# Hybrid transformer block on one core: a logarithm folded into the row of maxima, and a new order in the first unit

## What is computed

```python
x = x + attn_a(layernorm(x))   # 16 heads of width 64, full softmax, own residual and layer norm
x = x + ffn(layernorm(x))      # 128 -> 512 -> relu -> 128
x = x + attn_b(layernorm(x))   # 8 heads of width 128, rope, causal softmax
x = x + ffn(layernorm(x))
# attn_a: softmax over keys of (Q K^T) * 64**-0.5 * adaptive_scale[head], times V, times Wo
# attn_b: softmax over keys of (rope(Q) rope(K)^T) / 128, masked, times V, times Wo
```

## Time and profile before

| | |
|---|---|
| median of 3 runs | 1948.1 us (1947.27 to 1948.55) |
| profiled execution, its own time | 1947.32 us |
| its span | 1945.5 us |
| lead of phase A | up to 53.77 us, the first scores |
| phase A's steps | 53.77 to 1217.57 us, the end of the last exponential |
| dense layer and lead of phase B | to 1292.1 us |
| phase B's steps and the end | 1292.1 to 1945.5 us |
| busy, whole span | PE 96%, ACT 86%, POOL 83%, DVE 73% |
| mean granted clock of TensorE | 0.986 of full speed |

### The profile page before, as it was taken

How to read it: one execution, slowest core, us unless ns; L and a number is a source line. 1 busy time by engine, 2 the same in 40 slices (tenths; PEclk the granted TensorE clock), 3 DMA queues, 4 the chain that set the end, 5 groups by cost and what they waited for, 6 DMA issues and landing times.

```text
span 1945.5 us, 55434 instructions
## 1 busy us (share of the span) xinstructions
PE 1873.1 (96%) x23343; PEld 1268.5 (65%) x23343; DVE 1414.1 (73%) x2613; ACT 1674.5 (86%) x1919; POOL 1612.9 (83%) x1025
## 2 busy tenths in 40 slices
PE   4899999999999999999999999779999999999998
PEld 2566666666666666666666666547776777767766
DVE  7787778778777877877877864566767767667642
ACT  4799999999999999999999999747777777777774
POOL 3799999999999999999999999358787787886752
PEclk8899999999999999999999999889999999999999
DMA  6101101100100100100100100100000000000000
GB/s 145 35 11 26 34 14 23 35 15 21 35 18 18 34 19 18 35 18 18 35 18 18 34 2 2 55 1 2 2 1 2 2 2 1 2 1 2 2 2 23
DMA packets 45032, 37.94 MB, mean 19 GB/s; under 512 B 8304, under 2 KB 44144, under 8 KB 44528
## 3 DMA queue, kind: packets, MB, share of 16 engines
q1 hardware_dynamic: 44304, 34.00, 7.4%
q10 hardware_dynamic: 480, 0.39, 0.1%
HBM read 8.15 MB, written 1.05 MB: 5 GB/s over the span
## 4 chain that ended last, share of the span: by engine, by line
PE 84%; ACT 6%; DVE 4%; issue 3%; POOL 2%; ACTq 0%; POOLq 0%; DVEq 0%
PE ST L1612 10%; PE ST L1613 10%; PE RING L1473 6%; PE OO L1554 6%; PE OO L1556 6%; PE OO L1553 6%; PE OO L1473 4%; PE ST L1773 3%; PE ST L1778 3%; PE ST L1779 3%; PE ST L1780 3%; ACT PR L783 3%; PE OO L1800 2%; PE OO L1802 2%; PE OO L1804 2%
## 5 line engine op out<-in xcount | busy, mean ns | idle before, releaser
L609 POOL TENSOR_TENSOR PAB<-PR,PAB 128x1024 f16<-128x1024 f32 x342 | 728.8, 2131 | 51.4 <-ACT PAB L785 33.7
L785 ACT ACTIVATE PAB<-ST,lift_cols,exp_scale 128x1024 f16<-128x1024 f32 x512 | 654.5, 1278 | 0.0
L1081 DVE TENSOR_REDUCE maxes<-RING 128x1 f32<-128x512 f32 x661 | 439.8, 684 | 141.3 <-PE RING L1473 140.7
L783 ACT ACTIVATE PR<-ST,lift_cols,exp_scale 128x1024 f32<-128x1024 f32 x342 | 435.9, 1275 | 36.4 <-PE ST L1613 35.7
L1553 PE MATMUL OO<-VP,PAB 128*128 128x66 f16 x4096 | 447.2, 192 | 2.2 <-POOL PAB L609 2.2
L1554 PE MATMUL OO<-VP,PAB 128*128 128x64 f16 x4096 | 447.7, 194 | 0.0
L1556 PE MATMUL OO<-VP,PAB 128*128 128x66 f16 x4096 | 445.7, 192 | 0.0
L1553 PEld LDWEIGHTS OO<-VP,PAB 128*128 128x128 f16 x4096 | 380.7, 96 | 76.7 <-issue 14.7
L1554 PEld LDWEIGHTS OO<-VP,PAB 128*128 128x128 f16 x4096 | 377.5, 97 | 61.6
L1612 PE MATMUL ST<-QL,KH 128*128 128x512 f16 x1024 | 389.2, 380 | 4.1 <-ACT PAB L785 2.4
L1613 PE MATMUL ST<-QH,KL 128*128 128x512 f16 x1024 | 388.8, 380 | 0.0
(11 more groups left out here) (305 smaller groups left out, 4006.7 us busy)
## 6 DMA issues: line engine op xcount, KB each, us to landing
KH<-HS SPq DMA_DIRECT2D x124, 64.0 KB, 2.0
QL<-HS SPq DMA_DIRECT2D x64, 64.0 KB, 2.0
QL<-LS SPq DMA_DIRECT2D x64, 64.0 KB, 2.1
QH<-HS SPq DMA_DIRECT2D x64, 64.0 KB, 2.0
KL<-LS SPq DMA_DIRECT2D x62, 64.0 KB, 2.1
X<-in_L_attn_a_x SPq DMA_DIRECT2D x4, 256.0 KB, 3.9
SHARED<-in_rope_cos SPq DMA_DIRECT2D x1, 1024.0 KB, 5.0
SHARED<-in_rope_sin SPq DMA_DIRECT2D x1, 1024.0 KB, 7.1
```

Source lines behind the costliest of these rows:

```text
L609: pool.tensor_tensor(PB[:, s, :], PRA[g % PR_SLOTS], PA[:, s, :], ALU.subtract).then_inc(p_low_ready, 1)
L783: act.activation(PRA[g % PR_SLOTS], ST[step % 2][:, :], ACT.Exp, bias=lift_cols[:, 0:1], scale=scale)
L785: act.activation(PA[:, step % SLOTS_A, :], ST[step % 2][:, :], ACT.Exp, bias=lift_cols[:, 0:1], scale=scale).then_inc(sa.exps, 1)
L1081: dve.reduce_max(maxes[:, i // BLOCKS, i % BLOCKS:i % BLOCKS + 1], bank[:, :], X_AXIS).then_inc(sa.ring_taken, 1)
```

## The change

1. **No bias in the exponentials.** The column `lift_cols` is gone, and all 1024 exponentials of phase A and 640 of phase B are issued without a bias operand; the scale column stays.
2. **The logarithm goes into the row.** `take_rows` no longer computes `row * rowmask` but `(row + lift) * rowmask`, with `lift` a column of one value per head, `lifts` or `lifts_b` (one small DVE instruction each, computed once). It is a scalar_tensor_tensor in place of a tensor_tensor, 64 times in phase A and 32 times in phase B.
3. **`mask_operands` moves** from just ahead of `low_block` to just ahead of `bound_heads`, early in DVE's stream.
4. **First unit.** PE computes the scores of step 1 right after those of step 0. Values and maxima alternate: first half of the values, two maxima, second half, two maxima (item numbers 21, 22, 23, 24, 25, 26).

The diff, without the part that only moves the scores into a function of their own, `scores_a`:

```diff
-VALUES_LEAD = ROWS_LEAD + 1
+VALUES_LEAD = (ROWS_LEAD + 1, ROWS_LEAD + 4)
+MAX_LEAD = (ROWS_LEAD + 2, ROWS_LEAD + 3, ROWS_LEAD + 5, ROWS_LEAD + 6)
...
-                act.activation(PRA[g % PR_SLOTS], ST[step % 2][:, :], ACT.Exp, bias=lift_cols[:, 0:1], scale=scale)
+                act.activation(PRA[g % PR_SLOTS], ST[step % 2][:, :], ACT.Exp, scale=scale)
                 wait(act, sa.pv, g - SLOTS_A + 1)
-                act.activation(PA[:, step % SLOTS_A, :], ST[step % 2][:, :], ACT.Exp, bias=lift_cols[:, 0:1],
-                               scale=scale).then_inc(sa.exps, 1)
+                act.activation(PA[:, step % SLOTS_A, :], ST[step % 2][:, :], ACT.Exp, scale=scale
+                               ).then_inc(sa.exps, 1)
...
-            dve.memset(lift_cols[:, 0:1], LIFT)
-            dve.memset(lift_cols[:, 1:2], LIFT_B)
...
+                dve.scalar_tensor_tensor(lifts[:, :], qk_up[:, 0, :], LIFT, qk_up[:, 1, :], ALU.mult, ALU.mult)
...
+            mask_operands()
             bound_heads()
...
-            def take_rows(s, bank, item, dst):
+            def take_rows(s, bank, item, dst, lift):
 
                 dve.wait_ge(s.ring_put, item + 1)
                 rows = bank[0:BT, 0:P].unsqueeze(1).broadcast_to((BT, BT, P))
-                dve.tensor_tensor(dst.rearrange("p (a c) -> p a c", c=P), rows, rowmask[:, :, :],
-                                  ALU.mult).then_inc(s.ring_taken, 1)
+                dve.scalar_tensor_tensor(dst.rearrange("p (a c) -> p a c", c=P), rows, lift, rowmask[:, :, :],
+                                         ALU.add, ALU.mult).then_inc(s.ring_taken, 1)
...
-            mask_operands()
             low_block(1, 0, O[0])
...
             for half in range(2):
-                n = VALUES_LEAD + half
+                n = VALUES_LEAD[half]
                 take_values_a(0, half, RING3[n % 3], n)
-            for i in range(4):
-                n = VALUES_LEAD + 2 + i
-                take_max_a(RING3[n % 3], n, i, 1)
+                for i in (2 * half, 2 * half + 1):
+                    n = MAX_LEAD[i]
+                    take_max_a(RING3[n % 3], n, i, 1)
...
+                if g != 1:
+                    scores_a(g)
                 if g == 0:
+                    scores_a(1)
                     for half in range(2):
-                        values_a(half, VALUES_LEAD + half, 0)
-                    for i in range(4):
-                        max_a(1, i, VALUES_LEAD + 2 + i)
+                        values_a(half, VALUES_LEAD[half], 0)
+                        for i in (2 * half, 2 * half + 1):
+                            max_a(1, i, MAX_LEAD[i])
```

More of the change, by code:

```diff
@@ L299, in build @@
         exp_scale_b = sb("exp_scale_b", [P, HB])
-        lift_cols = sb("lift_cols", [P, 2])
+        lifts_b = sb("lifts_b", [P, HB])
         RAW = sb("RAW", [P, 4 * HA * DA])
@@ L317, in build @@
         exp_scale = sb("exp_scale", [P, HA])
+        lifts = sb("lifts", [P, HA])
         AT = sb("AT", [P, BLK])
@@ L893, in _ @@
                 act.wait_ge(sbb.scores, g + 1)
-                act.activation(PRB[g % PR_SLOTS_B][:, c0:BLK], SB[g % 2][:, c0:BLK], ACT.Exp,
-                               bias=lift_cols[:, 1:2], scale=scale)
+                act.activation(PRB[g % PR_SLOTS_B][:, c0:BLK], SB[g % 2][:, c0:BLK], ACT.Exp, scale=scale)
                 wait(act, sbb.pv, g - SLOTS_B + 1)
-                act.activation(PAH[:, g % SLOTS_B, c0:BLK], SB[g % 2][:, c0:BLK], ACT.Exp,
-                               bias=lift_cols[:, 1:2], scale=scale).then_inc(sbb.exps, 1)
+                act.activation(PAH[:, g % SLOTS_B, c0:BLK], SB[g % 2][:, c0:BLK], ACT.Exp, scale=scale
+                               ).then_inc(sbb.exps, 1)
                 for n, item in ITEMS_B[g]:
@@ L1210, in _ @@
                         nhead, nqb = divmod(u + 1, BLOCKS)
-                        take_rows(sa, bank, n, QH16[nhead % 2][0:BT, nqb * BLK:(nqb + 1) * BLK])
+                        take_rows(sa, bank, n, QH16[nhead % 2][0:BT, nqb * BLK:(nqb + 1) * BLK],
+                                  lifts[0:BT, nhead:nhead + 1])
                     elif item[0] == "project":
@@ L1341, in _ @@
                 take_max(sbb, RING3B[n % 3], n, qt, c, BLK if c < 1 else (qt + 1) * P, 2, i == 2 * BT - 1, 1)
-            take_rows(sbb, RING3B[(LEAD_B - 1) % 3], LEAD_B - 1, MROW[0:BT, 1, :])
+            take_rows(sbb, RING3B[(LEAD_B - 1) % 3], LEAD_B - 1, MROW[0:BT, 1, :], lifts_b[0:BT, 0:1])
             def last_ln(b):
@@ L1373, in _ @@
                     elif item[0] == "rows":
-                        take_rows(sbb, bank, n, MROW[0:BT, item[1] % 2, :])
+                        h = head + (item[1] < qb)
+                        take_rows(sbb, bank, n, MROW[0:BT, item[1] % 2, :], lifts_b[0:BT, h:h + 1])
                     elif item[0] == "project":
@@ L1576, in turned_a, with scores_a @@
                 ins.then_inc(sa.ring_put, 1)
+            def scores_a(g):
+                u, step = divmod(g, STEPS_A)
+                head, qb = divmod(u, BLOCKS)
+                hs = head % 2
+                q = slice(qb * BLK, (qb + 1) * BLK)
+                wait(pe, sa.exps, g - 1)
+                for j in range(2):
+                    keys = slice((2 * step + j) * P, (2 * step + j + 1) * P)
+                    tile = ST[step % 2][:, j * BLK:(j + 1) * BLK]
+                    pe.matmul(tile, KH16[hs][:, keys], QL16[hs][:, q], start=True, stop=False)
+                    ins = pe.matmul(tile, KL16[hs][:, keys], QH16[hs][:, q], start=False, stop=True)
+                ins.then_inc(sa.scores, 1)
             rows_item, turned_item = ROWS_LEAD, None
@@ L1603, in _ @@
                 head, qb = divmod(u, BLOCKS)
-                hs = head % 2
-                q = slice(qb * BLK, (qb + 1) * BLK)
                 if step == 0:
                     pe.wait_ge(sa.ring_taken, rows_item + 1)
-                wait(pe, sa.exps, g - 1)
-                for j in range(2):
-                    keys = slice((2 * step + j) * P, (2 * step + j + 1) * P)
-                    tile = ST[step % 2][:, j * BLK:(j + 1) * BLK]
-                    pe.matmul(tile, KH16[hs][:, keys], QL16[hs][:, q], start=True, stop=False)
-                    ins = pe.matmul(tile, KL16[hs][:, keys], QH16[hs][:, q], start=False, stop=True)
-                ins.then_inc(sa.scores, 1)
+                if g != 1:
+                    scores_a(g)
                 if g == 0:
+                    scores_a(1)
                     for half in range(2):
-                        values_a(half, VALUES_LEAD + half, 0)
-                    for i in range(4):
-                        max_a(1, i, VALUES_LEAD + 2 + i)
+                        values_a(half, VALUES_LEAD[half], 0)
+                        for i in (2 * half, 2 * half + 1):
+                            max_a(1, i, MAX_LEAD[i])
                 items = ITEMS_A[g]
```

19 lines of the change are left out of this document (11 added, 8 removed).

## The result

The changed kernel takes 1935.38 us (median of 5 runs, 1932.76 to 1938.3) against 1947.27 (5 runs, 1946.57 to 1948.55): a ratio of 0.9939, 95% interval 0.9926 to 0.9952, 11.9 us less. The profiled execution has an own time of 1935.38 and a span of 1933.6, again 1.8 outside the span. Predicted were 1937.0, a range of 1933.5 to 1943.0, and 11.0 us less. Of the 1.6 between 1937.0 and 1935.38, 0.8 is the median of the kernel before, which moved from 1948.1 to 1947.27.

The account below looks back on a forecast made before the run. PE was taken to bound the kernel, ACT only the light units. Terms -5.7 - 1.7 - 1.6 - 0.5 + 0.25 + 0.09 - 1.84 + 0 = -11.0 gave 1936.3 us, 1937.0 for the median; range 1933.5 to 1943.0.

Parts of the forecast that it names:

- ACT's step from 2.18 to 2.00, light units -5.7: Phase A: without bias ACT's step falls just below PE's 2.02, seven light units (11 to 59) gain 0.8 us each.
- that case: By the Trainium skill's figures ACT needs 2.08 a step; units 60 and 61 give 0.4 us less, sum -10.8.
- Units 60 and 61, -1.7: Last pair of heads, no projection: 1.2 us less in unit 60, 0.5 in unit 61; bounds -0.6 and -1.8.
- Last unit, -1.6: End of phase A: ACT and POOL set the pace, layer norm comes 1.6 us earlier; bounds -0.8 and -2.3.
- Phase B, -0.5: Only six exponentials after a table load in phase B's last unit gain, about 0.09 us each.
- `lifts_b` hidden: The small extra DVE instruction for phase B was said to be hidden, with no cost in the sum.
- Masks, -1.84: Lead: three mask instructions leave DVE's way before low_block, PE goes on 1.84 us earlier; bounds 0 and -1.84.
- Row, +0.25: take_rows costs 0.08 us more, felt at unit 0 and at two rows in phase B's lead.
- the slower rival: First scores of each unit: PE waits for the later row, 96 x 0.08 = 7.7 us, total 1954; chance 0.04.
- `lifts`, +0.09: The extra small instruction stands in a linked row of small ones on the path and costs 0.09 us.
- First unit, 0: New order of scores, values and maxima in the first unit: between -1.0 and +0.8 us, taken as 0.
- Between the phases, 0: Stretch from the table load to phase B's 11th step: predicted change 0.

Follow-up runs that it names:

- e1: The kernel before with the bias gone and the lift in take_rows, masks and first unit as they were: 1936.61 us against 1946.86, ratio 0.9949.
- e4: The changed kernel with a column of zeros as the bias of every exponential: 1945.42 us, ratio 0.9991 to the kernel before.
- e7: The changed kernel with a column of zeros as bias of the first exponential of each phase A step, none for the second: 1935.16 us.
- e5: The changed kernel with a column of zeros as the bias in phase B only: 1938.86 us, 1.4 above after_again.
- e6: The changed kernel with lifts_b computed in step 3 of unit 63 instead of unit 3: 1933.13 us, 4.4 below after_again.
- e10: The changed kernel with POOL's four small products put behind VectorE's first layer-norm shift after phase A: 1932.22 us against 1947.5, ratio 0.9919.
- e12: The changed kernel with lifts_b in the last unit, POOL behind the first shift, and useless matmuls before PE's waits between phases: 1928.84 us against 1947.41.
- e2: The kernel before with mask_operands moved, nothing else: 1945.13 us against 1946.86, ratio 0.9990.
- e3: The kernel before with the new order of the first unit, nothing else: 1947.35 us, ratio 1.0003.
- after_again: The changed kernel run once more, unedited, against the kernel before: 1937.5 us against 1947.42, ratio 0.9949.
- e9: The changed kernel with 8, 7, 5 and 4 useless matmuls ahead of PE's four waits between the phases: 1934.56 us against 1947.5, ratio 0.9933.

## Why the prediction was right, and where it was not

- *ACT's step from 2.18 to 2.00, light units -5.7*: right in mechanism and size (-5.9; seven times 0.83 or 0.84, the first at unit 11, the last at unit 59). e1 and e4 isolate it. The value 0.09 for a column, taken from scale and bias rows apart, held with one of the two gone. From the Trainium skill's figures ("ScalarE: Activation LUTs", section "What ACT_TABLE_LOAD costs") the prediction had estimated a step of 2.08 after; the trace has 2.00. e7, whose pair does take 2.08, shows that this would have cost the seven units nothing. The prediction's sum for that case was wrong in two ways: 0.4 off 11.0 leaves 10.6, not 10.8, and the last unit, where e7 loses 0.8, was left out.
- *Units 60 and 61, -1.7*: -2.0, the full bound and a little of unit 62 (0.2). POOL did not use up its lead.
- *Last unit, -1.6*: ACT's end came 2.0 earlier in the unit, POOL's 1.4. Which of the two counts was left half open in the prediction. The first layer after it begins 1.4 earlier when the shift is short (2.0 less the 0.6 of the table above), so it went by POOL; with the long shift the whole 2.0 is lost again, and 0.5 more.
- *Phase B, -0.5*: the step that failed. The 0.5 was for the last unit alone; there, e5 (-1.6) and e6, e10 and e12 (-2.0), the four executions without a late fall of the clock, differ by 0.4. The 2.8 between B10 and B310 had no term. I looked for ACT's idle time and, finding some in most steps, gave it cover. But a value product in each head waits for POOL, POOL for ACT's second exponential, and the trace showed it as a short wait of PE ([0.44 <-DVE AB], named after another engine). Idle time of ACT before a step is no cover for a latency inside it.
- *`lifts_b` hidden*: wrong by 1.1, see e6. I costed DVE's instruction by its columns and named no cover. A collision of this kind stood in the trace I used: `mask_ident` took 0.90 beside four POOL instructions in a row (L596, 24.51 to 29.01), and takes 0.22 where POOL is quiet.
- *Masks, -1.84*: e2 gives -1.7. In the traces of after and before PE goes on 2.4 earlier (27.43 against 29.79), and 1.75 of it reaches the first scores, the keys' DMA holding the rest. *Row, +0.25*: `take_rows` takes 0.73 rather than 0.67. PE waits for it once in phase A (1.0) and twice in phase B (0.5 before its maxima, 1.0 at its first scores), each 0.1 or less above the kernel before, and not at other units; the slower rival is out. *`lifts`, +0.09*, for which no row was given: in the kernel after the next instruction starts 0.09 after it (22.64 and 22.73). *First unit, 0*: e3 gives 0 (0.5 above the kernel before, inside the interval); step 2's scores stand at 63.53 in the kernel after, which is the forecast's 65.4 less the masks' 1.8.
- *Between the phases, 0*: measured +2.1. No term of the sum stood for it. 0.6 is POOL's later end, which belongs to the last unit's term; DVE meeting POOL can add 1.8 more, as in after_again; the 1.6 of the clock in this execution can't be put down to the change.

The misses of +1.0, +2.1 and -2.8 nearly cancel, which is luck and the reason why the total fits so well; a single total would not have shown them.

## What to carry to other kernels

Cut two traces at the same instructions and predict the pieces, not the total: here three wrong pieces summed to almost nothing. Take a second trace of each kernel before a difference of 1 us in a stretch with idle engines is explained: between the phases the clock alone moved executions of either kind by that much. A producer that is slower than its consumer costs nothing until the consumer's lead is used up, so half of a saving may bring all of the gain. A tiny VectorE instruction with all its inputs in SBUF is priced by what POOL is doing when it is issued, and by what POOL has ready after it: put it where POOL is idle (the masks) or where nothing waits for it (e6), or let POOL wait for it (e10).

## What was not expected of the hardware

- An 8-column instruction of DVE took 0.15 or 2.17 us, a 4-column one 0.90 or 2.75 to 2.77, at nearly the same place of the same kernel; the longer one covers several POOL instructions in a row (the rest of a subtraction and four small products).
- With work kept on PE through its waits the granted clock stayed at 0.83 and 1.00 where it had been 0.74 and 0.60 (e9, the two windows), and eight fp32 matmuls took 3.60 instead of 5.71.
- The exponentials' records grow while they follow each other without a break: 1.21 and 1.22 at the end of the last unit, 1.11 in the middle of phase A, while their starts stay 1.00 apart. In the kernel before they reached 1.48 at the end of the last unit, at a distance of 1.09. What grows is the record and not the time.
- Left open: why an execution has or has not a fall of the clock in its last 60 us (1.3 to 1.6 us), and why the shift is let in behind one POOL instruction in one execution and behind five in another.
